# A gated recurrent layer with an FFN: two weight-preparation passes move to GpSimd, and VectorE's order changes around them

## What is computed

```
pre = LN(x) @ W + b                         # 256 -> 4*256: i, f, o, z
i = 10*tanh((i_pre + input_bias)/10);  f = -softplus(f_pre);  o = sigmoid(o_pre);  z = tanh(z_pre)
for each step:  m' = max(f + m, i);  c = e^(f+m-m')*c + e^(i-m')*z;  n = e^(f+m-m')*n + e^(i-m')
                h = o * c / (n + 1e-6)
x1  = x + scale * h / rms(h)
w1, w2 = (q - 128) * scales                 # int32 codes, scales per group of 128 rows
out = x1 + 0.5 * (silu(LN(LN(x1))*gamma + beta) @ w1 + b1) @ w2 + ...)
```

## Time and profile before

| | us |
|---|---|
| median of 3 runs (321.66 to 321.97) | 321.74 |
| the profiled execution: its own time | 321.89 |
| its span, first to last instruction | 320.0 |
| TensorE busy in the span | 303.9 |
| VectorE busy | 267.4 |
| ScalarE busy | 229.7 |
| GpSimd busy | 118.1 |
| mean granted TensorE clock | 0.989 |

### The profile page before, as it was taken

How to read it: one execution, slowest core, us unless ns; L and a number is a source line. 1 busy time by engine, 2 the same in 40 slices (tenths; PEclk the granted TensorE clock), 3 DMA queues, 4 the chain that set the end, 5 groups by cost and what they waited for, 6 DMA issues and landing times.

```text
span 320.0 us, 4813 instructions
## 1 busy us (share of the span) xinstructions
PE 303.9 (95%) x1760; PEld 263.8 (82%) x1760; DVE 267.4 (84%) x474; ACT 229.7 (72%) x372; POOL 118.1 (37%) x126
## 2 busy tenths in 40 slices
PE   0999999999899997999999999999999999999996
PEld 0787788887898877988899888988899899899896
DVE  3998999999999999998969987888959899863531
ACT  3598966999599938489694978779593876941930
POOL 2162035002483179015920187014991156154000
PEclk9999998999999999799999999999999999999999
DMA  7990000000000020020000200010000100100101
GB/s 274 357 374 14 1 0 2 0 0 0 2 1 2 33 98 3 34 98 2 1 2 33 98 0 2 33 36 0 1 2 25 43 0 0 68 0 5 63 0 68
DMA packets 10951, 14.21 MB, mean 44 GB/s; under 512 B 688, under 2 KB 10160, under 8 KB 10672
## 3 DMA queue, kind: packets, MB, share of 16 engines
q1 hardware_dynamic: 10512, 13.12, 11.8%
q10 hardware_dynamic: 416, 0.79, 0.7%
HBM read 9.71 MB, written 4.19 MB: 43 GB/s over the span
## 4 chain that ended last, share of the span: by engine, by line
PE 45%; DVE 20%; issue 14%; POOL 12%; ACT 6%; DMA 3%; POOLq 0%; DVEq 0%; SPq 0%
PE mm_ps L221 7%; PE mm_ps L219 7%; PE mm_ps L220 7%; PE z_ps L220 6%; PE z_ps L219 6%; PE z_ps L221 6%; POOL rows L1034 3%; DVE rec L672 2%; DVE g L729 2%; DMA rows<-x 2%; POOL rec L1001 2%; DVE rows L737 2%; POOL g L1019 2%; DVE bn L742 2%; DVE rec L687 2%
## 5 line engine op out<-in xcount | busy, mean ns | idle before, releaser
L219 PE MATMUL z_ps<-w_hi,y_hi 128*128 128x256 f32 x248 | 71.3, 288 | 1.4 <-issue 1.4
L220 PE MATMUL z_ps<-w_lo,y_hi 128*128 128x256 f32 x248 | 70.4, 284 | 0.0
L221 PE MATMUL z_ps<-w_hi,y_lo 128*128 128x256 f32 x248 | 70.4, 284 | 0.0
L765 DVE TENSOR_TENSOR y_lo<-y,y_hi 128x512 fp32r<-128x512 f32 x64 | 43.2, 687 | 12.2 <-ACT y_hi L504 11.7
L501 ACT ACTIVATE y<-mm_ps,b_all 128x512 f32<-128x512 f32 x60 | 41.3, 688 | 13.4 <-PE mm_ps L288 9.8
L219 PEld LDWEIGHTS z_ps<-w_hi,y_hi 128*128 128x128 f32 x248 | 47.5, 191 | 1.9 <-issue 1.8
L220 PEld LDWEIGHTS z_ps<-w_lo,y_hi 128*128 128x128 f32 x248 | 47.2, 190 | 0.1
L221 PEld LDWEIGHTS z_ps<-w_hi,y_lo 128*128 128x128 f32 x248 | 47.1, 190 | 0.0
L1005 POOL TENSOR_TENSOR rrms<-meansq,minus_half 128x4 f32<-128x4 f32 x8 | 9.0, 1122 | 96.5 <-DVE meansq L723 96.5
L219 PE MATMUL mm_ps<-gt_hi,w_hi 128*128 128x512 f32 x108 | 43.2, 400 | 0.0
L220 PE MATMUL mm_ps<-gt_lo,w_hi 128*128 128x512 f32 x108 | 42.8, 396 | 0.0
(11 more groups left out here) (154 smaller groups left out, 669.4 us busy)
## 6 DMA issues: line engine op xcount, KB each, us to landing
out<-rows SPq DMA_DIRECT2D x15, 256.0 KB, 2.1
rows<-x SPq DMA_DIRECT2D x7, 512.0 KB, 6.4
q<-fc_q SPq DMA_DIRECT2D x2, 1024.0 KB, 12.1
s<-fc_scales SPq DMA_DIRECT2D x1, 1024.0 KB, 11.2
wg_raw<-fc_scales SPq DMA_DIRECT2D x1, 1024.0 KB, 11.1
wg_raw<-w_gates SPq DMA_DIRECT2D x1, 512.0 KB, 5.5
wg_raw<-w_gates ACTq DMA_DIRECT2D x1, 512.0 KB, 5.8
rows<-x ACTq DMA_DIRECT2D x1, 256.0 KB, 3.4
```

The costliest lines, as they stand in the source:

```text
L219: pe.matmul(dst, wh[w_at], ah[a_at], start=start, stop=False)
L220: pe.matmul(dst, wh[w_at], al[a_at], start=False, stop=False)
L221: return pe.matmul(dst, wl[w_at], ah[a_at], start=False, stop=stop)
L765: dve.tensor_tensor(y_lo[:, j], y[:, j % YBUFS], y_hi[:, j].bitcast(F32), ALU.subtract).then_inc(y_lo_done, 1)
```

## The change

- w1's low part (L830) leaves VectorE and goes to GpSimd, behind the halving of b2 and ahead of rms_root(0), with its wait for w1_rounded.
- w2's high part (L557) leaves ScalarE and goes to GpSimd, as a tensor_copy behind ln1_root(3) and ahead of rms_root(1), with its wait for w2_scaled.
- VectorE: ln1(3), sums and means, stands in the place of w1's low part; the second block of maximum(1) moves from behind ln1_means(3) to directly behind mean_square(0).
- VectorE: w2's low part moves from behind h_scaled(1) to ahead of it, and ln1(4), sums and means, from around mean_square(1) to behind h_scaled(1).

```diff
@@ ScalarE
             gates(3, range(0, 1))
             square_sums(1)
-            gates(3, range(1, 4))
-            act.wait_ge(w2_scaled, 1)
-            act.activation(w2_hi[:], w2_f, ACT.Copy).then_inc(w2_rounded, 1)
-            gates(3, range(4, GJ))
+            gates(3, range(1, GJ))
@@ VectorE
             h(0)
-            dve.wait_ge(w1_rounded, KD)
-            dve.tensor_tensor(w1_lo[:], w1_f, w1_hi[:].bitcast(F32), ALU.subtract).then_inc(w1_ready, 1)
+            ln1(3)
             maximum(1, range(0, 1))
             mean_square(0)
-            ln1_sums(3)
+            maximum(1, range(1, KD))
             dve.wait_ge(row_in, 16)
             h_scaled(0)
             residual(0)
             ln2_sums(0)
             ln2(0)
-            ln1_means(3)
-            maximum(1, range(1, KD))
             denominators(1, range(KD))
...
-            ln1_sums(4)
             mean_square(1)
-            ln1_means(4)
-            h_scaled(1)
             dve.wait_ge(w2_rounded, 1)
             dve.tensor_tensor(w2_lo[:], w2_f, w2_hi[:].bitcast(F32), ALU.subtract).then_inc(w2_ready, 1)
+            h_scaled(1)
+            ln1(4)
             residual(1)
@@ GpSimd
             pool.wait_ge(b2_in, 16)
             pool.tensor_scalar(b2_bc[:], b2_bc[:], 0.5, 0.0, ALU.mult, ALU.add).then_inc(b2_halved, 1)
+            pool.wait_ge(w1_rounded, KD)
+            pool.tensor_tensor(w1_lo[:], w1_f, w1_hi[:].bitcast(F32), ALU.subtract).then_inc(w1_ready, 1)
             rms_root(0)
             pool.wait_ge(x1_done, at(0, 1, 1))
             input_times_z(1)
             ln2_root(0)
             ln1_root(3)
+            pool.wait_ge(w2_scaled, 1)
+            pool.tensor_copy(w2_hi[:], w2_f).then_inc(w2_rounded, 1)
             rms_root(1)
```

## The result

The changed kernel takes 332.16 us (median of 4, 330.01 to 332.52) against 321.74 (median of 4, 321.66 to 321.97); the ratio is 1.031, with a 95% interval of 1.026 to 1.035. It is slower, inside the range forecast and 1.1 us above the predicted 331.1. The profiled execution took 331.88, its span is 329.9. The fences show picked rows; rows between them are left out.

The account below looks back on a forecast made before the run. VectorE's chain up to x_turned(5), where TensorE waits for g_low(2), was taken as the bound. Terms 4.3, 1.3, 0.9, 0.6, 1.8 and 0.5 sum to 9.4 us, giving 331.1 us, some 3% slower; range 325.0 to 334.0.

Parts of the forecast that it names:

- x_turned(5) is the meeting point: At x_turned(5) TensorE comes 2 us early and VectorE's g_low(2) decides, so lengthening VectorE's chain lengthens the run.
- Part 1: w1_lo on GpSimd holds VectorE off in denominators(0), ahead of divisor(0); gates(2, 0) and h(0) come 4.3 us later.
- two entries: GpSimd's w1_lo gets in between the two scans of denominators(0) or at the pause for the carry copy.
- Two of my signs: Expected in the profile: 5 us of ScalarE idle before L449, and TensorE's wait at L253 over 4 us.
- Part 1b: TensorE's clock drops behind the stop at gates(2, 0), before h_turned(0): 1.3 us counts, bounds 0 and 1.7 before cover.
- Part 2: Chunk 0's new order: scans hold off GpSimd's powers, 0.9 us on h_scaled(0) and 0.6 on g(0).
- Part 3: Around w2: GpSimd's copy costs VectorE 1.8 us, w2_lo holding the power before h_scaled(1) 0.5; ScalarE's freed pass gains nothing.
- The sum: Over the whole kernel, the terms of all parts add to 9.4 us, giving 331.1 us, some 3% slower.
- late entry (A): VectorE keeps GpSimd's w1_lo out until x_low(2), so only h(0) waits: 6.9 us, 328.6 us; chance 0.12.
- the hidden pass (C): The lead-in hides w1_lo where VectorE has nothing due: 3.6 us, 325.3 us; chance 0.09.
- the slow copy (B): GpSimd's copy of w2 is as slow as base's operations, 4.4 us: 2.5 more, 333.6 us; chance 0.10.
- no hold-off (D): Long GpSimd passes don't hold VectorE off, seen at denominators(0)'s second scan: 321.3 us, within 0.2%; chance 0.09.

Follow-up runs that it names:

- the pass alone: The kernel before with only w1's low part moved to GpSimd, behind the halving of b2: 327.48 us, ratio 1.019.
- The memset: The changed kernel with w1's low part not computed, GpSimd filling it with zeros at the same place in its queue: 325.88 us, ratio 1.013.
- the run with the old order back: The changed kernel with VectorE's order as in the kernel before, both passes still on GpSimd: 328.27 us, ratio 1.021.
- the order alone: The kernel before with only VectorE's new order of chunk 0, the order around w2 and both passes as before: 323.84 us, ratio 1.006.
- the run with the order alone: The kernel before with VectorE's whole new order, around chunk 0 and w2, both passes on their old engines: 326.99 us, ratio 1.016.
- the earlier g_low(2): The kernel before with, in chunk step 4 alone, g_high(2) ahead of x_normalised(5) and g_low(2) ahead of numerators(3): 322.14 us, ratio 1.001.

## Why the prediction was right, point by point

- *What bounds the kernel.* Right in what it did: VectorE's chain decides, the 1.37 us for w2_ready are worth nothing (with w2_lo behind h_scaled(1) fc2(0) waits again and x_turned(5) is still earlier), and the shift at residual(1) is the shift of the end. The step "x_turned(5) is the meeting point" was too narrow: the chain meets TensorE again at h_turned(3), for x_low(5).
- *Part 1, 4.3.* Measured 4.3 in the change, the second scan held at the joint; the pass alone gave 5.5 at x_turned(5) with the clock's part. The memset shows that its reading does it. I took one of two entries as equal in price; it was the first. Two of my signs came out short, ScalarE's idle time (4.38, not 5) and TensorE's stop (3.84, not over 4). gates(2, 0) did start 4.3 later; TensorE's work ahead of it ended 0.7 later than in the execution of the kernel before.
- *Part 1b, 1.3.* Measured 1.15, and 1.15 to 1.17 in the two other runs with a stop of 3.8 us; but 2.17, over my upper bound of 1.7, in the run with the old order back, whose stop was 4.58, the length that I had priced. The price was right for a stop that came out shorter, which is in part luck. The granted clock of 40 to 45 us is 0.71 in the changed kernel and 1.00 before:

```profile
40.00:45.00 5.00, 4.19 (x12) 3.15 (x13) 4.80 (x14) 4.05 (x8) 0.00 (x0) 0.71 0.01 2
```

- *Part 2, 0.9 and 0.6.* Measured 0.94 and 0.61, and 1.5 at g_turned(0) with the order alone. 0.3 more came between g(0) and w2's scaling: the eight transposes of g_turned(0), behind a stop of 1.69 instead of 0.56 us, took 1.97 instead of 1.69. That it belongs to the change isn't shown, since kernels that are equal up to there differ by more (40.99 to 42.05).
- *Part 3, 1.8 and 0.5.* Measured 1.7 and 0.57. The cast's row is 2.29 with some 0.5 of waiting in it (y_low(0, 2), issued at 77.00, lasts to 77.69), near the lower of my ends of 1.9 and 4.4, the one taken. One thing was missing: I costed ScalarE's freed pass at nothing and didn't see that without it the new place of w2_lo makes VectorE wait 3.37 us (the run with the order alone). The sum wasn't touched, since the change makes both edits.
- *The sum, 9.4.* Measured 9.56 at x_turned(5) behind the 0.41 of the first loads; the medians differ by 10.4, with an interval of 8.5 to 11.4. The rivals fall by these rows: late entry (A) and the hidden pass (C) by the second scan's 5.57, the slow copy (B) by 2.29, no hold-off (D) by both.

The parts tried by themselves add up to about what the change costs: ratios 1.019, 1.006 and 1.006 for w1_lo, w2_hi and chunk 0's order, and 0.57 us around w2, which is 0.002, give 1.033; the change gave 1.031. At x_turned(5) the shifts are 5.50, 1.16, 1.84 and 0.57, in all 9.1 of the 9.56. Both agree within the spread, which is also as much as they can show.

## What to carry to other kernels

An idle engine is no free place for a pass if its reading holds up the engine that is relieved, as GpSimd's did here: look at which instructions run on the other one in that window and how many of their operands lie in SBUF, and at who waits for them. A pass of 2.28 us taken from VectorE cost 5.5 us, because it was given to GpSimd where VectorE was in a chain for which ScalarE was waiting. Where another engine's small result is needed next, put an instruction with one SBUF operand behind its trigger; and where an engine's chain is the bound, take what nothing waits for out of its way first, which was worth 2.5 us here together with the earlier g_low(2). Before you explain a few tenths of a microsecond from one profile, look how far profiles of kernels that are equal up to that point differ.

## What the runs showed of the hardware that I had not expected

- Cutting GpSimd's pass into eight doesn't let VectorE through at full speed. They alternate, and eight pieces took 12.26 us where one took 5.52 with 1.0 of waiting in it.
- TensorE's clock behind a stop isn't the same from run to run. Of the ten profiled executions with a stop of 2.0 to 2.2 us before x_turned(5), nine had a granted clock of 0.66 in the 5 us behind it and took 192.3 to 192.5 us from there to the end; one had 1.00 and took 191.0. The length of the eight transposes (1.22 to 1.84 us) says less: four executions had 1.22 to 1.29, and only one of them kept its clock. A stop of 2.36 us at h_turned(3) was followed by 1.00 as well. What decides isn't shown here.
- The changed kernel's four runs spread over 2.5 us, with mean granted clocks of 0.984 at 330.01 and 0.974 at 332.45 and 332.52. A part of a few tenths of a microsecond therefore shows in the rows and not in the time.
